# An RWKV layer on one Trainium2 core: read-out in two row groups, and one PSUM bank in turn for three users

## The reference, cut to what is computed

```python
def step(s, rkvw):
    r_t, k_t, v_t, w_t = rkvw
    a = k_t[:, :, :, None] * v_t[:, :, None, :]
    out = jnp.einsum('bhk,bhkd->bhd', r_t, u * a + s)
    return (a + w_t[:, :, :, None] * s, out)
...
m = jnp.mean(a4, axis=-1, keepdims=True)
var = jnp.mean((a4 - m) ** 2, axis=-1, keepdims=True)
att = ((a4 - m) * jax.lax.rsqrt(var + EPS)).reshape(b, l, E) * gn_w + gn_b
x = x + att * g @ Wo.T
```

## Time and profile before

| | |
|---|---|
| median of 3 runs | 1747.12 us (1746.57 to 1752.07) |
| the profiled execution | 1747.81 us |
| its span | 1745.7 us, 42924 instructions |
| TensorE busy | 1611.0 us, 92% (17600 passes) |
| weight loads | 1198.2 us, 69% |
| VectorE, POOL, ScalarE busy | 964.8, 644.0, 555.6 us (55, 37, 32%) |
| granted TensorE clock, mean | 0.96 |

### The profile page before, as it was taken

One profiled execution on the slowest core, in us unless ns is written; L12 is line 12 of the kernel. 1 busy time (PEld: TensorE's weight loads), 2 busy tenths in 40 slices (PEclk: granted clock), 3 DMA queues, 4 the chain that ended last, 5 costly groups with the idle time before them and its releaser, 6 DMA issues.

```text
span 1745.7 us, 42924 instructions
## 1 busy us (share of the span) xinstructions
PE 1611.0 (92%) x17600; PEld 1198.2 (69%) x17600; DVE 964.8 (55%) x1942; ACT 555.6 (32%) x898; POOL 644.0 (37%) x540
## 2 busy tenths in 40 slices
PE   4878899999989998999989999899989999999765
PEld 3657676777767676777757777676767777676533
DVE  3273656656565664766546566556646665655412
ACT  1122333333332332424323343333334342332221
POOL 3142524425352432535234253424425352433310
PEclk8979899999999999999999999999989999999888
DMA  6000101101010100101001110101101010100100
GB/s 257 1 27 19 39 15 30 37 27 41 14 51 13 49 17 25 39 14 53 13 25 38 28 40 14 49 15 31 34 25 39 14 53 13 34 20 17 46 25 12
DMA packets 65316, 58.96 MB, mean 34 GB/s; under 512 B 24256, under 2 KB 57408, under 8 KB 64128
## 3 DMA queue, kind: packets, MB, share of 16 engines
q1 hardware_dynamic: 65152, 56.41, 10.5%
HBM read 35.36 MB, written 8.39 MB: 25 GB/s over the span
## 4 chain that ended last, share of the span: by engine, by line
PE 73%; DVE 12%; issue 8%; ACT 3%; POOL 3%; SPq 1%; DMA 0%; POOLq 0%; DVEq 0%; ACTq 0%
PE pair L901 27%; PE pair L909 18%; PE pair L955 4%; PE at_ps L844 3%; PE att_ps L892 3%; PE at_ps L837 3%; PE pair L935 2%; PE pair L979 2%; PE pair L917 2%; DVE kT L491 2%; POOL cen L407 2%; DVE x L578 2%; PE pair L981 2%; PE att_ps L864 1%; PE att_ps L883 1%
## 5 line engine op out<-in xcount | busy, mean ns | idle before, releaser
L901 PE MATMUL pair<-x,wts 128*128 128x256 f32 x2048 | 462.1, 384 | 6.8 <-ACT kT L707 5.3
L901 PEld LDWEIGHTS pair<-x,wts 128*128 128x128 f32 x2048 | 386.0, 191 | 71.3 <-ACT kT L707 9.7
L381 POOL TENSOR_TENSOR x<-x,xnT 128x1024 f32<-128x1024 f32 x80 | 178.6, 2232 | 289.6 <-DVE x L578 289.6
L578 DVE SCALAR_TENSOR_TENSOR x<-pair,vecs,sx 128x256 f32<-128x256 f32 x320 | 132.5, 477 | 219.2 <-PE pair L955 219.2
L718 ACT ACTIVATE at<-at_ps 64x512 f32<-64x512 f32 x256 | 151.4, 592 | 217.2 <-PE at_ps L844 215.4
L901 PE MATMUL pair<-yT,wts 128*128 128x256 f32 x512 | 119.6, 393 | 5.2 <-DVE yT L662 5.2
L909 PE MATMUL pair<-wts,yT 128*128 128x512 f32 x256 | 118.0, 605 | 5.6 <-POOL yT L419 5.6
L909 PE MATMUL pair<-wts,cen 128*128 128x512 f32 x256 | 122.7, 624 | 0.0
L909 PE MATMUL pair<-wts,sx 128*128 128x512 f32 x256 | 114.1, 599 | 1.3 <-ACT cen L702 1.1
L901 PEld LDWEIGHTS pair<-yT,wts 128*128 128x128 f32 x512 | 99.4, 197 | 22.5 <-issue 8.8
L461 DVE SCALAR_TENSOR_TENSOR bonv<-rT,vecs,kT 128x128 f32<-128x128 f32 x128 | 39.0, 367 | 136.2 <-ACT rT L707 77.5
(11 more groups left out here) (134 smaller groups left out, 2616.7 us busy)
## 6 DMA issues: line engine op xcount, KB each, us to landing
rm<-rst SPq DMA_DIRECT2D x1024, 12.0 KB, 1.8
xu<-in_x SPq DMA_DIRECT2D x16, 512.0 KB, 4.4
wts<-in_wts SPq DMA_DIRECT2D x8, 1024.0 KB, 13.3
s<-in_s SPq DMA_DIRECT2D x128, 64.0 KB, 1.8
x<-in_x SPq DMA_DIRECT2D x16, 512.0 KB, 4.4
out<-sx SPq DMA_DIRECT2D x16, 512.0 KB, 3.1
prev<-in_prev SPq DMA_DIRECT2D x32, 4.0 KB, 4.3
maa<-in_maa SPq DMA_DIRECT2D x1, 448.0 KB, 3.7
```

The costliest lines, as they stand in the source:

```text
L381: gp.tensor_tensor(t, t, xnT[:, :, :, 1:L1].rearrange("p g b t -> p (g b) t"), ALU.add).then_inc(x5_ready, 1)
L578: last = ve.scalar_tensor_tensor(seqs(x5[q], g), ps[:, :, g * L:(g + 1) * L], vecs[:, vec, g:g + 1], seqs(sx, g), ALU.add, ALU.mult)
L901: last = pe.matmul(ps[:, g // 2, TB * (g % 2):TB * (g % 2 + 1)], wts[:, m, k, g * P:(g + 1) * P], source[:, k, :], start=(k == 0), stop=(k ...
```

## The change

1. The read-out of `at` is cut by input rows: for each head two matmuls, over rows 0 to 63 and 64 to 127, each writing 64 tokens. `att_ps` is now one tile of two banks, one for each half of the tokens, both with all units of both sequences. The `s0` product is two matmuls, one for each bank. `at` keeps only the two diagonal blocks, and `evict` is one copy on 128 rows.
2. `at_ps` is one bank instead of two. `kt`, `kv` and `aT` no longer use `att_ps[b]`, but one bank `kv_ps` in turn, and wait for each other's readers. The order is changed for that on TensorE, ScalarE and VectorE.
3. `c1v_0` stands ahead of `chain0b` on VectorE, and `bon0` ahead of `rch0b` on POOL.

With its core (left out: the counts of the `setup` semaphore):

```diff
@@ -55,17 +55,17 @@
     "kt0": 0, "kt1": 0, "kv0": 0, "kv1": 0, "attb1": -1, "attb0": 0, "aT1": -1, "aT0": 0}
 
 
-PE_ORDER = ["mixW", "V7", "kt0", "wv.0", "aT1", "kv0", "A0", "wv.1", "z", "V0", "mixK", "c02_1", "A1", "mixG",
+PE_ORDER = ["mixW", "V7", "wv.0", "aT1", "A0", "kt0", "wv.1", "kv0", "z", "V0", "mixK", "c02_1", "A1", "mixG",
             "V1", "decay", "A2", "k.0", "k.1", "yT", "V2", "g.0", "g.1", "c1v_1", "A3", "mixR", "wo.0", "V3",
-            "kt1", "wo.1", "aT0", "kv1", "mixV", "A4", "r.0", "r.1", "V4", "x2T", "A5", "v.0", "v.1", "xT",
+            "kt1", "wo.1", "kv1", "mixV", "A4", "r.0", "r.1", "aT0", "V4", "x2T", "A5", "v.0", "v.1", "xT",
             "V5", "c02_0", "A6", "kk.0", "kk.1", "c1v_0", "V6", "rr.0", "rr.1", "h", "A7"]
-ACT_ORDER = ["kt0", "att1", "E0", "gn_square", "z", "gn_std", "E1", "decay", "E2", "k", "yT", "g", "vtm1",
+ACT_ORDER = ["att1", "E0", "kt0", "gn_square", "z", "gn_std", "E1", "decay", "E2", "k", "yT", "g", "vtm1",
              "E3", "kt1", "E4", "r", "x2T", "E5", "v", "xT", "E6", "att0", "kk", "vtm0", "rr", "h", "E7"]
-DVE_ORDER = ["mixW", "attb1", "chain1", "gn_sum", "kv0", "wv", "gn_var", "mixK", "c02_1", "gn_rec", "mixG",
+DVE_ORDER = ["mixW", "attb1", "chain1", "gn_sum", "gn_var", "wv", "kv0", "mixK", "c02_1", "gn_rec", "mixG",
              "chain1b", "ln1_stats", "ln1", "g", "c1v_1", "mixR", "attb0", "wo", "ln2_stats", "kv1", "mixV",
-             "ln2", "chain0", "x2T", "c02_0", "xT", "chain0b", "c1v_0"]
+             "ln2", "chain0", "x2T", "c02_0", "xT", "c1v_0", "chain0b"]
 POOL_ORDER = ["mixW", "gn_sub", "rch1", "wv", "mixK", "gn_scale", "mixG", "c02_1", "rch1b", "ln1_stats",
-              "yT", "bon1", "mixR", "ln2_stats", "mixV", "rch0", "c02_0", "rch0b", "bon0"]
+              "yT", "bon1", "mixR", "ln2_stats", "mixV", "rch0", "c02_0", "bon0", "rch0b"]
 SP_ORDER = ["x", "M1", "M2", "out", "x2", "M3", "M4", "M5", "M6", "M7", "M0"]
 
 
@@ -146,7 +146,7 @@
         rst = sb("rst", [P, NB, G, RST])
         rm = [sb(f"rm{p}", [P, HG, RMW]) for p in range(2)]
         s0 = [sb(f"s0{q}", [P, P]) for q in range(2)]
-        at = sb("at", [P, HG, L])
+        at = sb("at", [P, HG, 64])
         vtm = [sb(f"vtm{b}", [P, 2 * E]) for b in range(NB)]
 
         axn = sb("axn", [P, G * NB * L1])
@@ -167,8 +167,9 @@
         yo = sx2[:, :, :].rearrange("p g t -> p (g t)")
 
         pair = [ctx.enter_context(nc.psum_tensor(f"pair{p}", [P, 2, 512], F32)) for p in range(2)]
-        at_ps = [ctx.enter_context(nc.psum_tensor(f"at_ps{q}", [P, 512], F32)) for q in range(2)]
-        att_ps = [ctx.enter_context(nc.psum_tensor(f"att_ps{b}", [P, E], F32)) for b in range(NB)]
+        at_ps = ctx.enter_context(nc.psum_tensor("at_ps", [P, 512], F32))
+        att_ps = ctx.enter_context(nc.psum_tensor("att_ps", [P, 2, NB, G, 64], F32))
+        kv_ps = ctx.enter_context(nc.psum_tensor("kv_ps", [P, E], F32))
 
         (sel_in, lora_in, setup, x_in, prev1_in, prev0_in, xres_in, out_done,
          stat1, aggr1, eps1, rstd1_ready, xn_ready, prev1_put, xnT_ready, sx_ready, u_ready, h_ready,
@@ -613,13 +612,13 @@
                     b = int(name[-1])
                     ve.wait_ge(read_done, a.count(UNITS, 4 * (b + 1)))
                     ve.wait_ge(bon, a.count(2 * NBON, NBON * (b + 1)))
-                    t = bonv[:, b, :, :].rearrange("p g t -> p (g t)")
-                    ve.tensor_tensor(t, att_ps[b][:, :], t, ALU.add).then_inc(attT_ready, 1)
+                    t = bonv[:, b, :, :].rearrange("p g (c t) -> p c g t", c=2)
+                    ve.tensor_tensor(t, att_ps[:, :, b, :, :], t, ALU.add).then_inc(attT_ready, 1)
                 elif name in ("kv0", "kv1"):
                     b = int(name[-1])
                     ve.wait_ge(kv_done, a.count(2, b + 1))
                     ve.tensor_tensor(kvs[:, :].rearrange("p (g c) -> p g c", g=G),
-                                     att_ps[b][:, :].rearrange("p (g c) -> p g c", g=G),
+                                     kv_ps[:, :].rearrange("p (g c) -> p g c", g=G),
                                      headall[:, :].unsqueeze(1).broadcast_to([P, G, P]), ALU.mult)\
                       .then_inc(kvs_ready, 1)
                 elif name == "gn_sum":
@@ -713,11 +712,8 @@
                 ac.wait_ge(levels_done, at_.count(UNITS, n + 1))
                 if at_.past(UNITS, n):
                     ac.wait_ge(read_done, at_.count(UNITS, n))
-                for c in range(2):
-                    rows_ = slice(64 * c, 64 * c + 64)
-                    last = ac.activation(at[rows_, :, rows_],
-                                         at_ps[n % 2][rows_, :].rearrange("p (h t) -> p h t", h=HG), ACT.Copy)
-                last.then_inc(at_ready, 1)
+                ac.activation(at[:, :, :], at_ps[:, :].rearrange("p (h t) -> p h t", h=HG), ACT.Copy)\
+                  .then_inc(at_ready, 1)
 
             def stage(name, i, at_):
                 a = c = at_.plus(AHEAD[name])
@@ -774,13 +770,13 @@
                     ac.wait_ge(kt_done, a.count(2, b + 1))
                     if a.past(UNITS, 4 * b):
                         ac.wait_ge(read_done, a.count(UNITS, 4 * b))
-                    ac.activation(kvs[0:64, :], att_ps[b][0:64, :], ACT.Copy).then_inc(kt_ready, 1)
+                    ac.activation(kvs[0:64, :], kv_ps[0:64, :], ACT.Copy).then_inc(kt_ready, 1)
                 elif name in ("att0", "att1"):
                     b = int(name[-1])
                     ac.wait_ge(aT_done, a.count(2, b + 1))
                     if a.past(1, 0):
                         ac.wait_ge(xr_ready, a.count(1, 0))
-                    ac.activation(att[:, b, :], att_ps[b][:, :], ACT.Copy).then_inc(att_ready, 1)
+                    ac.activation(att[:, b, :], kv_ps[:, :], ACT.Copy).then_inc(att_ready, 1)
                 elif name == "gn_square":
                     ac.wait_ge(cen_ready, c.count(1, 1))
                     ac.activation(sq, kk, ACT.Square).then_inc(sq_ready, 1)
@@ -822,9 +818,9 @@
                 if g == 0:
                     pe.wait_ge(kchain, at_.count(2 * NK, NK * (b + 1)))
                 pe.wait_ge(rm_in[p], at_.count(16 * HG * UNITS // 2, 16 * HG * (n // 2 + 1)))
-                if at_.past(UNITS, n - 1):
-                    pe.wait_ge(at_ready, at_.count(UNITS, n - 1))
-                out = at_ps[p][:, :].rearrange("p (h t) -> p h t", h=HG)
+                if at_.past(UNITS, n):
+                    pe.wait_ge(at_ready, at_.count(UNITS, n))
+                out = at_ps[:, :].rearrange("p (h t) -> p h t", h=HG)
                 r4, r16 = R4C - R16C, 0
                 for odd in range(2):
                     for s in range(1, 4):
@@ -849,10 +845,12 @@
             def turn_k(at_, b):
 
                 pe.wait_ge(kchain, at_.count(2 * NK, NK * (b + 1)))
-                if at_.past(2, b - 1):
-                    pe.wait_ge(att_ready, at_.count(2, b - 1))
+                if b == 0 and at_.past(2, 0):
+                    pe.wait_ge(att_ready, at_.count(2, 0))
+                if b == 1:
+                    pe.wait_ge(kvs_ready, at_.count(2, 1))
                 for g in range(G):
-                    last = pe.transpose(att_ps[b][:, g * P:(g + 1) * P], k64[:, 64 * g:64 * g + P], ident[:, :])
+                    last = pe.transpose(kv_ps[:, g * P:(g + 1) * P], k64[:, 64 * g:64 * g + P], ident[:, :])
                 last.then_inc(kt_done, 1)
 
             def outer(at_, b):
@@ -861,37 +859,45 @@
                 pe.wait_ge(vtm_ready, at_.count(2, b + 1))
                 for g in range(G):
                     v = bass.AP(vtm[b], g * 2 * P, [[2 * E, 64], [64, G], [48, 2], [1, S]])
-                    last = pe.matmul(att_ps[b][:, g * P:(g + 1) * P], kvs[0:64, g * P:(g + 1) * P], v,
+                    last = pe.matmul(kv_ps[:, g * P:(g + 1) * P], kvs[0:64, g * P:(g + 1) * P], v,
                                      start=True, stop=True)
                 last.then_inc(kv_done, 1)
 
             def turn_att(at_, b):
 
                 pe.wait_ge(attT_ready, at_.count(2, b + 1))
+                pe.wait_ge(kvs_ready, at_.count(2, 2))
+                if b == 1:
+                    pe.wait_ge(att_ready, at_.count(2, 1))
                 for g in range(G):
-                    last = pe.transpose(att_ps[b][:, g * P:(g + 1) * P], bonv[:, b, g, :], ident[:, :])
+                    last = pe.transpose(kv_ps[:, g * P:(g + 1) * P], bonv[:, b, g, :], ident[:, :])
                 last.then_inc(aT_done, 1)
 
             def read_out(at_, n):
 
                 b, g = n // G, n % G
-                o = att_ps[b]
+                o = att_ps[:, :, b, g, :]
                 if g == 0:
                     pe.wait_ge(kvs_ready, at_.count(2, b + 1))
                     pe.wait_ge(rchain, at_.count(2 * NR, NR * (b + 1)))
+                    if at_.past(2, b - 1):
+                        pe.wait_ge(attT_ready, at_.count(2, b - 1))
                 pe.wait_ge(s0_in[n % 2], at_.count(64, 16 * (n // 2 + 1)))
```

(17 more changed lines are left out.)

12 lines of the change are left out of this document (5 added, 7 removed).

## The result

The changed kernel took **1850.93 us** (median of 4 runs, 1848.62 to 1853.57) against 1748.43 us of the kernel before (4 runs, 1746.57 to 1752.07): ratio **1.0584, 95% interval 1.0558 to 1.061**. It is slower, as forecast, but by 102 us where 79 were forecast, and 3 us above the end of the range. The profiled execution took 1848.62 us with a span of 1846.5, 100.8 more than before.

A forecast was written before the change was run, and what follows sets the result against it. The prediction took TensorE, busy 92% of the span, as the bound. Its terms, 58.8 - 4.6 + 44.8 - 16.3 - 4 = +78.7 on 1747.81 us, gave 1826 us, range 1773 to 1848 us.

The forecast's parts named there:

- V0 stands, 14 steps: TensorE waits ahead of V0 for VectorE's kv0 behind gn_var and wv, 4.2 us in steps 2 to 15: +58.8 us.
- clock behind it: TensorE's granted clock halves behind each standstill ahead of V0, losing 3.2 us in each of 14 steps: +44.8 us.
- `zt` wait gone: TensorE's 0.33 us wait for zt ahead of c02_1 is swallowed by the standstill ahead of V0: -4.6 us.
- read-out: Narrow passes on half the rows run side by side, 0.17 us gained per unit, s0 split free: -16.3 us.
- `c1v_0` early: h waits less for L601 behind chain0b in steps -1 and 0, 0 to 12 us, taken as -4 us.
- Rival B: In the read-out the halves don't run side by side: gain vanishes (1842 us) up to a loss (1890 us); chance 0.07.
- A: Rival: TensorE stalls ahead of V0 but the clock stays, 1781 us; chance 0.13.
- C: Rival: V0 is not held up, kvs ready within 2.1 us, so the change only gains, 1727 us; chance 0.08.
- D: Rival: the change doesn't do what it says, neither stall nor read-out gain, 1747 us; chance 0.03.

The follow-up runs named there:

- e3: The changed kernel with ten needless matmuls of 256 columns on TensorE ahead of V0 in steps 2 to 15, filling the stall: 1807.8 us, ratio 1.0333.
- e1: The changed kernel with VectorE's kv0 put back right behind gn_sum, ahead of wv and gn_var, nothing else: 1754.08 us, ratio 1.0019.
- e2: The kernel before with only VectorE's order of the change (gn_sum, gn_var, wv, kv0): 1872.21 us, ratio 1.0702.
- e5: e1 with the read-out's narrow passes reordered, all heads over rows 0 to 63 first, then over rows 64 to 127: 1763.16 us, ratio 1.0088.
- e12: e1 with kt0 and kv0 ahead of A0 in the first two steps, six mask copies released earlier, x loaded behind M1's copies: 1725.8 us.
- e7: The kernel before with only the load of x moved behind M1 in SyncE's order: 1734.3 us, ratio 0.9921.
- e4: The kernel before with only c1v_0 ahead of chain0b on VectorE and bon0 ahead of rch0b on POOL: 1726.85 us, ratio 0.9867.

## Why the prediction was right or wrong

The terms of the sum against what the traces show, in us of span, after against before:

| term | on record | measured |
|---|---|---|
| V0 stands, 14 steps | +58.8 | +61.4 |
| clock behind it | +44.8 | +50.6 (e3: 43 to 48) |
| `zt` wait gone | -4.6 | -3.8 (13 waits) |
| read-out | -16.3 | -2.2 |
| `c1v_0` early, start (to V7 of block 1) | -4 | +0.8 |
| loop's jumps | 0 | -4.4 (23.3 to 18.9) |
| clock behind the jumps | 0 | -1.7 |
| tail, behind V7 of block 15 | 0 | +2.1 |
| sum | +78.7 | +102.8, against 100.8 |

The clock behind the jumps is counted over the 8 us behind each: 0.79, 0.50, 0.58, 0.58, 0.58 after, 0.59, 0.57, 0.57, 0.57, 0.52 before.

**The stall** was right in mechanism and size: 6.55 us from the end of `wv.1` to V0 (6.3 on record), 2.1 of cover, 4.38 of standstill (4.2), 14 times. e1 and e2 show that the order of VectorE alone makes it.

**The clock** was right in mechanism; e3 shows it by holding the clock up. The size holds as well. I had taken the loss behind a jump, 3.2 us, and called 3.4 the upper bound. e3, which measures the time that comes back, gives 3.1 to 3.4 a stall; the count by the clock gives 3.6, but counted in that way the jump at 893.41 has 3.4 (8 us at 0.57), and there the same work took 3.2 us longer. So the 50.6 is 3 to 7.5 us too high, which is also where the sum's excess of 2 us can come from.

**The `zt` wait** is gone as said, but it was 3.8 us in 13 waits, and it went for another reason. It is gone in e1 too, where nothing stalls: `kv0` now stands between `wv.1` and `z`, and its 1.1 us cover the chain from `wv.1` to ScalarE's `zt` (4.5 us from the end of `wv.1` to `c02_1` in e1, 3.7 before).

**The read-out is the step that failed**, by 14.1 us. On record: "The s0 product in two matmuls streams the same columns; ... so the two more cost between 0 and 0.26 us; I take 0, since part of that 0.26 is the switch to narrow tiles." It cost 0.17 in the `s0` passes and 0.05 in `kvs`, 0.22 a unit, near the end of that bound that I did not take. The row that decides was among those I read: the `kvs` product's two passes of 64 columns took 0.26 us, no less than the 0.22 us of the `s0` product's two passes of 128, and I set it aside. Rival B had the gain vanish too, but because the halves don't run side by side, and that is not what happened: the narrow passes gained 0.19, and the profile has them overlapping in either order (e5). Each unit but one lost 0.03 us net. V2 gained 0.37, and so the term comes to (9052 - 9187) ns x 16 = -2.2 us. I had left V2 out because `g.0` behind it waits for ScalarE's kT; in e1 and e12 that wait is gone. The one eviction of `at_ps` for two (0.60 us for 1.20) takes ScalarE's work ahead of kT down, which fits, but it was not tried alone. I had booked that edit at nothing.

**`c1v_0` early** was mis-sized twice. Alone it is worth 20 us: 10.8 in the start, where 0 to 12 was on record and 4 taken, and 9.7 at the jumps (6.6 of standstill, the rest the clock behind it), which the forecast did not touch. "Nobody on TensorE was near" was true, but SyncE's queue was: the move shifts a 512 KB load from ahead of the jump's instruction packet to behind it, and e7 shows that moving this load away gains 14.6 us. Inside the full change most of the start's gain is lost again to `A0` waiting ahead of `kt0`, of which I had written only that it "hangs on the masks".

**What hid itself**: e1 pays 13.3 us at `A2` for the masks, the changed kernel almost nothing (0.4 us between 206 and 1640 us). TensorE, late by a stall and slow behind it, gives the copies time. That goes far to explain why removing the stall gained 98.0 us and not the 112 of the first two rows (61.4 + 50.6 - 13.3 = 98.7); the clock's term, a few us too high, is another part of it.

Of the rivals none came about: A (the clock stays) is refuted by the 0.53 behind V0, C (V0 not held up) by the 15 waits, D by the time. The range was drawn too narrow for its own bounds: 5.6 for the stall, 2.8 for the clock and 16.3 for the read-out above 1826 make 1850.7, not 1848, and the measured 1850.93 is all but at that sum.

## What to carry to other kernels

When an engine's list is rearranged, follow each moved entry to the one that waits for it, and count the whole chain of whatever now stands ahead; one list entry cost 98 us here. Price a split of a matmul by its weight loads: with 128 weight columns a pass cost the same here at 16, 64 and 128 streamed columns, so splitting tokens in two doubled it, and only the narrow-weight part gained. And look at what each queue does while a loop jumps: a large load issued just ahead of it held the instruction packet back.

## What the hardware showed that I had not expected

- A jump of the loop leaves TensorE standing 3.0 to 3.2 us with no load beside it (e7) and up to 5.0 us while a 512 KB load keeps the DMA engines 88% busy (before). In all 70 jumps of the 14 kernels TensorE starts again 1.6 to 1.8 us after the end of one 16 KB packet of the instruction queue, and x only shifts when that packet starts.
- The length of a standstill does not tell what the clock loses behind it. Over the 8 us behind, it was 0.79 at all five of e7's jumps (2.97 to 3.15 us) and 0.57 behind one of 5.0 us before, but also 0.57 behind one of 3.28 us in e4 and 0.79 behind one of 3.58 us in the changed kernel. What decides stays open.
- Needless matmuls in a standstill made the kernel 43 us faster (1850.93 to 1807.8), since the granted clock stayed at 1.00.
- SyncE's issue of eight small copies took 4.9 us in some stages and up to 6.9 us in others (e1, M2), on the same kind of copy. What it depends on stays open.
